# A three-stage language-model tower: first embeddings and conv 1 issued sooner on TensorE, and two of GpSimd's deviations exchanged

## The reference, cut to what matters

```python
# 1 field
amps   = emb[ids]                                            # look-up
h      = gelu(conv1d(onehot(ids), w1, b1, pad=3))            # conv 1, 64 -> 128, 7 taps
h      = gelu(conv1d(h, w2, b2, pad=2))                      # conv 2, 128 -> 64, 5 taps
ctx    = sigmoid(conv1d(h, w3, b3, pad=1))                   # conv 3, 64 -> 1, 3 taps
amps   = amps * ctx
z      = (positions - center(shapes[ids])) / width_s         # for 4 scales s
basis  = sum_s exp(-z*z/2) * cos(phase + 2*pi*z) * amp_scale * scale_weights[s]**2
field  = einsum('bsp,bsd->bpd', basis, amps)
# 2 attention: a complex linear recurrence over a layer norm
h = field + state_space(layernorm(field))
# 3 experts: top 1 of 8 over a layer norm
H = gelu(layernorm(h) @ W1 + b1)
h = h + prob[top] * (H @ Wd[top] + bd[top])
```

## Time and profile before

| | |
|---|---|
| median of 3 runs | 111.67 us (111.58 to 112.59) |
| the profiled execution | 111.52 us |
| its span | 109.6 us (1.9 us lie around it) |
| TensorE busy | 100.5 us (92%), 723 matmuls |
| VectorE busy | 90.0 us (82%) |
| ScalarE busy | 70.8 us (65%) |
| GpSimd busy | 51.0 us (47%) |

### The profile page before, as it was taken

The page is one execution under the profiler, slowest core; times in us unless marked ns, Lnnn a source line. Parts: engine busy times, 40 slices in busy tenths (PEclk is TensorE's granted clock), DMA queues, the critical chain, the costliest instruction groups (busy, mean ns, idle before and its releaser), DMA issues.

```text
span 109.6 us, 2018 instructions
## 1 busy us (share of the span) xinstructions
PE 100.5 (92%) x723; PEld 64.3 (59%) x723; DVE 90.0 (82%) x230; ACT 70.8 (65%) x126; POOL 51.0 (47%) x101
## 2 busy tenths in 40 slices
PE   5979999999999978869899999999999799999970
PEld 2356785364434576347567477876696476776640
DVE  0359999999999949999999599678999956199892
ACT  4604599999999999999869438454758513551000
POOL 7798998899980007205509426256005000000670
PEclk9999999999999999999999999999999999999999
DMA  3999700000000100000000000000000000000044
GB/s 91 269 233 408 283 0 0 3 0 0 6 0 4 5 0 0 0 0 6 0 0 0 0 6 0 0 0 0 0 0 9 0 0 0 0 0 0 0 96 96
DMA packets 4313, 4.15 MB, mean 38 GB/s; under 512 B 3280, under 2 KB 3536, under 8 KB 4176
## 3 DMA queue, kind: packets, MB, share of 16 engines
q1 hardware_dynamic: 4160, 3.92, 12.5%
q10 hardware_dynamic: 144, 0.12, 0.4%
HBM read 3.50 MB, written 0.52 MB: 37 GB/s over the span
## 4 chain that ended last, share of the span: by engine, by line
PE 42%; ACT 38%; DVE 8%; DMA 4%; issue 4%; POOL 2%; ACTq 0%; DVEq 0%
PE pair L1080 14%; ACT wave L476 8%; PE bank L1042 7%; ACT bell L466 7%; ACT bell L470 5%; ACT L425 5%; DMA ids<-x 4%; DVE pair L819 3%; PE hid_pair L1053 3%; PE pair L951 3%; ACT angle L514 3%; PE pair L921 2%; ACT h L460 2%; PE hid_pair L1063 2%; ACT dist L455 2%
## 5 line engine op out<-in xcount | busy, mean ns | idle before, releaser
L379 POOL TENSOR_SCALAR var_eps<-mean_var 128x4 f32<-128x4 f32 x8 | 3.7, 458 | 33.0 <-DVE mean_var L747 33.0
L819 DVE COPY_PREDICATED pair<-later,pair 128x256 f32<-128x256 int32 (+3 forms) x30 | 12.3, 409 | 5.3 <-PE pair L1080 4.6
L921 PE MATMUL pair<-warm 128*128 128x512 bf16 x53 | 13.3, 380 | 0.0
L732 DVE SCALAR_TENSOR_TENSOR bell<-bell,scale_w,wave 128x512 f32<-128x512 f32 x16 | 10.8, 743 | 0.0
L1080 PE MATMUL pair<-wd_high,H_high 128*128 128x512 f32 x32 | 10.8, 418 | 0.0
L921 PE MATMUL hid_pair<-warm 128*128 128x512 bf16 x30 | 9.0, 455 | 1.3 <-POOL warm L298 1.3
L1080 PE MATMUL pair<-wd_low,H_high 128*128 128x512 f32 x32 | 10.0, 394 | 0.0
L395 POOL TENSOR_TENSOR angle<-picked,prob 128x256 f32<-128x256 f32 x3 | 1.8, 613 | 17.2 <-DVE prob L843 17.2
L521 ACT ACTIVATE bell<-hid_pair,sm 128x512 f32<-128x512 f32 x8 | 5.0, 680 | 7.2 <-PE hid_pair L1053 7.2
L675 DVE TENSOR_TENSOR wave<-dist,inv_width 128x2048 f32<-128x2048 f32 x4 | 9.3, 2356 | 0.0
L965 PE MATMUL pair<-h,w_sb 128*64 128x512 f32 x40 | 9.1, 597 | 0.0
(11 more groups left out here) (166 smaller groups left out, 226.1 us busy)
## 6 DMA issues: line engine op xcount, KB each, us to landing
ids<-x SPq DMA_DIRECT2D x2, 512.0 KB, 5.7
posb<-positions SPq DMA_DIRECT2D x1, 768.0 KB, 8.1
wd_sb<-wd SPq DMA_DIRECT2D x1, 512.0 KB, 9.1
out<-angle SPq DMA_DIRECT2D x3, 128.0 KB, 2.0
st_sb<-state SPq DMA_DIRECT2D x1, 328.0 KB, 8.3
w_sb<-w SPq DMA_DIRECT2D x1, 256.0 KB, 6.6
posb<-positions SPq DMA_DIRECT2D x1, 256.0 KB, 6.6
w_sb<-w SPq DMA_DIRECT2D x1, 160.0 KB, 8.0
```

The lines of the kernel that those rows point to most:

```text
L732: ins = dve.scalar_tensor_tensor(out=bell[:, g, part], in0=bell[:, g, part], scalar=scale_w[:, s:s + 1], in1=wave[:, g, part], op0=ALU.mul ...
L819: return dve.copy_predicated(held[:, :, 0:n, 0, 0:D], repeat(later[:, g, 2 * h + rows.start:2 * h + rows.stop, first:first + n], 3, D), he ...
L921: pe.matmul(bank[free], warm[:, 0:P], warm[:, :], start=True, stop=True)
```

## The change

Three things change.

1. On TensorE the three fillers between the shape look-ups and `embeddings(0)` go, and the three behind `embeddings(0)` become two.
2. Conv 1 is issued for one group at a time: part 0 and part 1 of group 0, then of group 1, and so on.
3. On GpSimd `inv_std(1, 0)` stands ahead of `inv_std(0, 2)`.

```diff
@@ GpSimd @@
             inv_std(0, 0)
             inv_std(0, 1)
+            inv_std(1, 0)
             inv_std(0, 2)
-            inv_std(1, 0)
             inv_std(0, 3)
@@ TensorE @@
-            keep_warm(3, 7)
             embeddings(0)
-            keep_warm(3, 7)
+            keep_warm(2, 7)
             pe.wait_ge(s_onehot, 2)
-            conv1((0, 1))
-            conv1((2, 3))
+            for g in range(G):
+                conv1((g,))
             conv2(0)
```

## The result

| | before | after |
|---|---|---|
| median, runs beside each other | 112.12 us (111.58 to 112.59, 4 runs) | 117.12 us (116.45 to 117.20, 3 runs) |
| ratio | 1 | 1.043, 95% interval 1.034 to 1.052 |
| profiled execution, its span | 111.52, 109.6 us | 117.2, 115.3 us |
| granted TensorE clock, mean over the span | 1.00 | 0.97 |

The account below looks back on a forecast made before the run. Bounds: ScalarE from the start, handing up to 1.45 us to VectorE, then the chain around 60 us and TensorE without slack behind 63 us. Terms -0.50 and +2.95 on the median 111.67 made 114.1 us, range 112.9 to 115.4.

Parts of the forecast that it names:

- The three stretches: Start (ScalarE waits for conv 1), middle (VectorE waits 1.45 us at 40.68), around 60 us (turn(0, 2) to turn(1, 0)).
- Parts 1 and 2: Start: fewer fillers and conv 1 by group bring ScalarE's gelu 1.1 us sooner; VectorE's z leaves -0.50 us.
- conv 2, 0.8 sooner: Start, TensorE: conv 2 comes 0.8 us sooner and is not late for the 0.50 us gain.
- Part 3: GpSimd's exchange: offset of (0, 2) 3.0 us later, turn(1, 0) moves by 2.95 us; term +2.95, bounds 2.7 to 3.9.
- 0.1 for what a small VectorE instruction may hold up: GpSimd, end of the exchange: allowance of 0.1 us that puts the offset of (0, 2) at 62.2 instead of 62.10.
- Rival 4: TensorE's clock falls in the 2.9 us of idleness or at the start: 1.9 us, 116.0 us; chance 0.05.
- Rivals 2 and 3: Power of (1, 0): 2, caught by VectorE's scan, 115.0 us, chance 0.08; 3, scan waits for it, 114.9 us, 0.05.
- Rival 1: TensorE's stretch behind 62.7 us absorbs the exchange's delay, leaving only the head's gain: 111.2 us; chance 0.10.
- rival 3: VectorE's scan waits for GpSimd's power; offset of (0, 2) at about 62.9, 0.8 us more: 114.9 us; chance 0.05.
- the forecast's own range: Total time without the rivals: 113.5 to 114.7 us, from head 0 to 0.8 and exchange 2.7 to 3.2; chance 0.72.

Follow-up runs that it names:

- e1: Kernel before with only the changed start (fewer fillers, conv 1 by group), GpSimd's order as before: 111.69 us, ratio 0.998; 111.21 us at full clock.
- e6: Kernel before with conv 1 by group and three fillers at embeddings(0), one ahead and two behind: 111.25 us at full clock; 7 of 12 fell.
- e4: Kernel before with only the fillers' change, conv 1 in pairs as before: ratio 0.997; 111.05 us at full clock.
- e2: Kernel before with only GpSimd's exchange, TensorE's start as before: 116.8 us, ratio 1.041.
- e12: e8 with 16 instead of 14 fillers at TensorE's very start: 110.84 us, ratio 0.993 against the kernel before.
- e5: Kernel before with GpSimd's exchange and 20 instead of 5 fillers ahead of turn(0, 2): 116.37 us; 114.79 and 114.85 us at full clock.
- e8: Kernel before with e6's start, normalise(1, 0) ahead of scan(1), two instead of six fillers ahead of turn(1, 0): 110.94 us, ratio 0.995.

## Why the prediction was wrong

**Bounds of the kernel: right.** The three stretches, the wait of 1.45 us on VectorE, ScalarE's queue behind normalise(0, 2) and TensorE's lack of slack behind 63 us all held: `turn(1, 0)` moved by 5.79 us and the span by 5.7.

**Parts 1 and 2, "-0.50 us": right at full clock, wrong in what earned it.** e1 measured -0.50 there and e6's trace shows the numbers of the forecast (square(0) held by z, 0.96 us of VectorE's wait left). But e4 has it without grouping. The barrier that I passed over in one clause ("conv 2, 0.8 sooner") is the one that decides for grouping alone. In the kernel as changed the term was +1.02 in place of -0.50. Nearly all of the difference is conv 1 at the fallen clock, 9.34 us for 7.90; the one-hot table that was 0.4 us late kept conv 1 from starting as early as forecast.

**Part 3, "+2.95 us": the mechanism right, the size 3.3 to 3.4.** The failing item is "0.1 for what a small VectorE instruction may hold up": the offset fell into VectorE's `turn_back` (L787, 62.31 to 63.60) and ended 0.06 us behind it, 0.73 us long. In before an offset beside L787 (52.21 to 53.50) took 0.47; I had that row before me and did not use it for this place:

```profile
53.09 0.47 POOL L386 TENSOR_TENSOR offset<-negated,rstd 128x4 f32<-128x4 f32 x1
```

**Rival 4, the clock: the step that failed.** The sum had the fallen clock at nothing, and the rival had 0.05, at 1.9 us, as one event. It happened twice: all three runs of after have 0.97, two stretches at half clock, and the trace has one on conv 1 and one behind TensorE's wait. My ground against it was that TensorE had done nothing for 3.4 us at the end with the clock still full. That row can't carry this: the clock falls not when the idle time begins but well into it. In after, 63.0 to 64.8 us still has 1.00, 1.2 to 3.0 us behind the last filler, and 65.0 on has 0.50. In e2's trace the idle time began at 60.73 and the clock fell at 63.6, 0.5 us ahead of the next matmul. The end of the kernel shows the same. Before, the clock fell after the span was over, while in e12, whose program ends in the same way, it fell inside the span, with the last matmul over at 105.5 us:

```profile
109.60:110.90 1.30, 0.00 (x0) 0.00 (x0) 0.00 (x0) 0.00 (x0) 0.00 (x0) 1.00 0.00 0
111.00:111.70 0.70, 0.00 (x0) 0.00 (x0) 0.00 (x0) 0.00 (x0) 0.00 (x0) 0.50 0.00 0
```

```profile
105.50:107.90 2.40, 0.02 (x1) 0.00 (x0) 1.36 (x5) 0.00 (x0) 0.41 (x1) 1.00 0.61 136
108.20:109.00 0.80, 0.00 (x0) 0.00 (x0) 0.00 (x0) 0.00 (x0) 0.00 (x0) 0.50 0.04 8
```

Over the fourteen kept traces the fall comes 2.5 to 5.1 us behind the last matmul, inside the span in six of them. That the earlier trace rows showed 3.4 us at full clock was thus the chance of one execution. The price of the fall in the gap was 1.1 us (e2 against e5) to 1.33 (the trace of after). At the start one stretch at half clock cost 1.1 to 1.9 us of span (e1, e4, e6, e8), and two in a row 2.6 to 2.7 (e1, e8). With the clock kept, e1 and e5 together make 111.7 - 0.5 + 3.3 = 114.5 us, an estimate and inside my range: it is the clock that took the time out of it.

The Trainium skill (TensorE: Matmul & The Clock Gate, section "HAM oscillation — how this bites in real kernels") describes a kernel in which the waits for data between bursts of matmuls make each next burst start at half clock. The trace agrees with 0.50 behind the wait. Had I weighed that page against the earlier trace rows, I would have given the rival more than 0.05.

**Rivals 2 and 3, the scan.** The power of (1, 0) ran from 60.09 to 61.12, and the scan that started inside it at 60.30 took 1.22 us, as ever. So neither held up the other. The Trainium skill's rule that GpSimd would hold the port pair for the whole instruction (SBUF — State Buffer, section "SBUF: two separate sides") is not borne out for this power; its other side is, for var_eps, which ended at 61.54 with the scan (61.52), and for the offset.

**Rival 1, no cost on the path: out.** TensorE took back next to nothing: `turn(1, 0)` came 5.79 us later and the span grew by 5.7.

**Slips in the sums.** They change nothing. In rival 3 the offset at 62.9 is 0.7 us after 62.2 and not 0.8. In the forecast's own range no gain at the start with 3.2 us for the exchange makes 114.9 us and not 114.7. And `upright(3)` at 63.97 for 61.00 is 2.97 us, of which I took 2.95.

Two things stay open. All three runs of after in the table had 0.97, so they seem to have fallen at the start too, where e1 with the same start fell in 4 of 12. And what makes one execution of a kernel fall at its start and the next one not is not shown by any run here.

## What to carry to other kernels

When two calls of a serial engine are exchanged, price what each one's readers have queued behind them: here the wait that was removed (1.17 us on VectorE) was covered by fillers, and the one put in its place stood on TensorE's path and cost 3.3 us. Ask of each new wait of TensorE whether it will cost its clock too, and take no comfort from an idle time at the end of a trace, whose consequence lies behind the last row. Where fillers are removed, run often enough to count how many executions keep the clock: medians of 111.7 us hid a gain of 0.5 us in two thirds of the runs and a loss of 0.8 to 2.5 us against that in the rest.

## What the runs showed of the hardware that I had not expected

- In both traces the clock's fall comes near the end of TensorE's idle time of 3.36 us (2.9 and 3.1 us into it), so the work behind the wait pays: transposes of 0.69 instead of 0.44 us, fillers at 2.57 instead of 1.46 us for six.
- The same kernel keeps or loses the clock at its start from run to run: before lost it in 13 of 95 runs, and a thinned start with 14 first fillers in 22 of 60.
- A power on GpSimd and a scan on VectorE overlap when the power starts 0.21 us ahead. A var_eps that starts inside the scan and an offset inside `turn_back` end with VectorE's instruction (0.44 and 0.73 us long instead of 0.23 and 0.20). It depends on what VectorE runs: the power of (0, 2) started at 61.82 inside normalise (L754, 61.44 to 62.40) and took its usual 1.03.
